# Last walk of a graph network kernel: a sixth of the one-hots is made one stage earlier, and the blocks' loads change engine

## The reference

```python
def gat_conv(x, W, att_src, att_dst, b, src, dst):
    n = x.shape[0]
    h = (x @ W).reshape(n, H, C)               # H = 2 heads, C = 64
    loops = jnp.arange(n, dtype=src.dtype)
    s = jnp.concatenate([src, loops])
    d = jnp.concatenate([dst, loops])
    a_s = jnp.einsum('nhc,hc->nh', h, att_src)
    a_d = jnp.einsum('nhc,hc->nh', h, att_dst)
    e = jax.nn.leaky_relu(a_s[s] + a_d[d], NEG_SLOPE)
    m = jax.ops.segment_max(e, d, num_segments=n)
    p = jnp.exp(e - m[d])
    denom = jax.ops.segment_sum(p, d, num_segments=n)
    alpha = p / (denom[d] + 1e-16)
    out = jax.ops.segment_sum(h[s] * alpha[:, :, None], d, num_segments=n)
    return out.reshape(n, H * C) + b
...
h = jax.nn.relu(gat_conv(x, W1, ...) + x @ Wsk1 + bsk1)
out = gat_conv(h, W2, att_src2, att_dst2, b2, src, dst) + h @ Wsk2 + bsk2
...
x = _layernorm(x + out)
```

## Time and profile before

| | us |
|---|---|
| median of 3 runs | 5302.19 |
| lowest and highest run | 5302.08, 5308.24 |
| span of the profiled execution | 5296.6 |
| busy: POOL, DVE, PE, ACT | 3515.2, 3404.7, 3373.0, 2334.8 |
| the last walk, from its first one-hot to the last instruction | some 393 |

### The profile page before, as it was taken

One profiled execution on the slowest core, in us unless ns is written; L12 is line 12 of the kernel. 1 busy time (PEld: TensorE's weight loads), 2 busy tenths in 40 slices (PEclk: granted clock), 3 DMA queues, 4 the chain that ended last, 5 costly groups with the idle time before them and its releaser, 6 DMA issues. The chain is left out here.

```text
span 5296.6 us, 96022 instructions
## 1 busy us (share of the span) xinstructions
PE 3373.0 (64%) x21145; PEld 2475.7 (47%) x21146; DVE 3404.7 (64%) x12799; ACT 2334.8 (44%) x6751; POOL 3515.2 (66%) x4335
## 2 busy tenths in 40 slices
PE   0027677677768869996959999962000899531566
PEld 0027666576756534441216666742000777420465
DVE  6984466554448857777848888863260888651777
ACT  0015466576657734442327888840000444200466
POOL 3870288676745567763748888867576555574999
PEclk9999899899989989997979999985555999855788
DMA  2123466598989862210113444435111999451576
GB/s 75 39 74 107 138 207 207 167 270 240 262 220 286 265 245 53 53 45 18 38 52 125 138 143 141 140 110 140 36 41 38 299 293 293 148 145 42 172 223 200
DMA packets 593103, 784.79 MB, mean 148 GB/s; under 512 B 138946, under 2 KB 362870, under 8 KB 592330
## 3 DMA queue, kind: packets, MB, share of 16 engines
q1 hardware_dynamic: 431734, 533.20, 32.7%
q0 software_dynamic: 62848, 112.43, 8.8%
q10 hardware_dynamic: 98328, 137.22, 7.1%
HBM read 470.23 MB, written 317.95 MB: 149 GB/s over the span
## 5 line engine op out<-in xcount | busy, mean ns | idle before, releaser
L2884 POOL TENSOR_SCALAR n_hot<-node_of,d_krel 128x256 f32<-128x256 f32 x396 | 381.1, 982 | 65.4 <-ACTq L2940 65.4
L1332 ACT ACTIVATE n_r<-n_r,n_shift,n_rstd 128x128 f32<-128x128 f32 x784 | 321.6, 480 | 79.0 <-POOL n_shift L1323 73.0
L1047 PE MATMUL e_bank<-x_rows,e_hot 128*128 x1584 | 197.6, 282 | 231.3 <-DVE e_hot L1020 184.1
L1003 POOL DMA_INDIRECT x_rows<-x,d_other_i x196 | 260.3, 1328 | 118.6 <-POOLq L102 59.2
L2912 PE MATMUL n_bank<-h_rows,n_hot 128*128 x1584 | 240.2, 320 | 146.1 <-POOL n_hot L2884 146.1
L684 POOL DMA_INDIRECT agg<-e_msg,e_put_i x196 | 194.2, 991 | 165.9 <-DVEq L713 114.6
L2912 PEld LDWEIGHTS n_bank<-h_rows,n_hot 128*128 128x128 f32 x1584 | 227.9, 231 | 159.1 <-issue 159.0
L1047 PEld LDWEIGHTS e_bank<-x_rows,e_hot 128*128 128x128 f32 x1584 | 185.4, 192 | 243.7 <-issue 243.7
L1332 ACT ACTIVATE n_o<-n_y_ps,n_shift,n_rstd 128x128 f32<-128x128 f32 x784 | 292.6, 453 | 13.0 <-POOL n_shift L1619 12.8
L615 POOL DMA_INDIRECT agg_dst<-e_rows,e_put_i x196 | 195.2, 996 | 101.9 <-issue 59.4
L2505 POOL TENSOR_TENSOR n_u<-n_u 128x512 f32<-128x512 f32 x98 | 124.5, 1271 | 205.7 <-DVE n_u L2452 205.7
(11 more groups left out here) (522 smaller groups left out, 11631.2 us busy)
## 6 DMA issues: line engine op xcount, KB each, us to landing
n_ag<-agg_dst SPq DMA_DIRECT2D x196, 264.0 KB, 2.9
n_hs<-h SPq DMA_DIRECT2D x196, 264.0 KB
n_xs<-x SPq DMA_DIRECT2D x196, 256.0 KB, 4.4
agg_dst<-e_ev SPq DMA_DIRECT2D x196, 132.0 KB
y<-n_o ACTq DMA_DIRECT2D x98, 264.0 KB, 2.7
e1a_fed<-y SPq DMA_DIRECT2D x196, 132.0 KB
m<-e1a_ev SPq DMA_DIRECT2D x196, 132.0 KB
e1b_fed<-m SPq DMA_DIRECT2D x196, 132.0 KB
```

The lines of the kernel that those rows point to most:

```text
L1003: pool.indirect_dma_start(out=rows[:, c, 0:fetched], out_offset=None, in_=table, in_offset=bass.IndirectOffsetOnAxis(ap=e.other_i[:, c:c + ...
L1047: ins = pe.matmul(bank[:, bass.ds(to + h * width, summed)], hot[:, s, k, h * P:(h + 1) * P], flat_rows[:, bass.ds(row, summed)], start=Fal ...
L1332: ins = act.activation(out[:, g, 0:D], r[:, g, :], ACT.Identity, bias=shift[:, g:g + 1], scale=rstd[:, g:g + 1])
L2884: ins = pool.tensor_scalar(hot[:, i // STEPB % HOTS, i % STEPB, :], keep.node_of[:, :], e.krel[:, i:i + 1], None, ALU.is_equal)
```

## The change

In the first part of `edge_shares` VectorE also makes, for each batch n, the one-hot of the batch's first step, in a ring of three buffers (`SPARES`). SyncE stores it to `spare_hots` in DRAM. In `walk_last` GpSimd skips the first step of each batch, SyncE fetches it into `hot[:, s, 0, :]` once `steps_done` frees the place, and TensorE also waits for `spare_in`. SyncE has no other work there: `load` and `close` are ScalarE's, whose lags are `close` 6, `begin` 2, `load` 0, `take_root` 7, `store` 9, `apply` 8.

```diff
 edge_shares, SyncE and VectorE:
+                    def store_spare(n):
+                        sp.wait_ge(spare_made, n + 1)
+                        sp.dma_start(spare_hots[n], spare[:, n % SPARES, :]).then_inc(spare_out[n % SPARES], 16)
...
+                        if n >= SLICES_IN:
+                            store_spare(n - SLICES_IN)
+                    for n in range(slices - SLICES_IN, slices):
+                        store_spare(n)
+                    for n in range(SPARES):
+                        sp.wait_ge(spare_out[n], 16 * (slices // SPARES))
...
+                        if n >= SPARES:
+                            dve.wait_ge(spare_out[n % SPARES], 16 * (n // SPARES))
+                        dve.tensor_scalar(spare[:, n % SPARES, :], keep.node_of[:, :], on_dst.krel[:, n * STEPB:n * STEPB + 1], None,
+                                          ALU.is_equal).then_inc(spare_made, 1)
 walk_last, GpSimd, TensorE, SyncE and ScalarE:
                     if i % STEPB == 0:
                         pool.wait_ge(steps_done, i + STEPB)
+                        continue
...
+                        pe.wait_ge(spare_in[s], turn * 16 + 16)
                         pe.wait_ge(hot_ready, turn * HOTS + s + 1)
...
-                run(sp, (0, load), (4, close))
+                with sp.Fori(0, BATCHES // HOTS) as turn:
+                    for s in range(HOTS):
+                        sp.wait_ge(steps_done, turn * (HOTS * STEPB) + (s + 1) * STEPB)
+                        sp.dma_start(hot[:, s, 0, :], spare_hots[bass.ds(turn * HOTS + s, 1)].squeeze(0)).then_inc(spare_in[s], 16)
...
+                def load(turn, s):
+                    upto(act, owned, turn, s, SLOT)
+                    act.dma_start(rows_of(hs, s), pair_rows(h4, turn, s)).then_inc(h_in[s % SLOT], 16)
+                    upto(act, begun, turn, s, SLOT, 2)
+                    act.dma_start(rows_of(ss, s), pair_rows(s4, turn, s)).then_inc(s_in[s % SLOT], 16)
...
+                    act.wait_ge(steps_done, ends[2 * (s % 2) + 1] & 511)
+                    act.sem_inc(closed, 1)
...
-                run(act, (0, begin), (PAST, begin_past), (5, take_root), (7, store), (6, apply))
+                run(act, (6, close), (2, begin), (0, load), (PAST + 2, begin_past), (7, take_root), (9, store), (8, apply))
```

More of the change, by code:

```diff
@@ L2602, with edge_shares @@
 SUMMED = D + GAT_HEADS
-def edge_shares(nc, keep, name, e, on_dst, krel_rows, h, a_nodes, values_edges, shares_edges, rows, share):
+SPARES = 3
+def edge_shares(nc, keep, name, e, on_dst, krel_rows, h, a_nodes, values_edges, shares_edges, rows, share, spare_hots):
     values = 2 * GAT_HEADS
@@ L2619, in edge_shares @@
             hot = ph.sb("hot", [P, 2, 2, SLICE * P], BF16)
+            spare = ph.sb("spare", [P, SPARES, TILE])
+            spare_made, spare_out = ph.sem("spare_made"), [ph.sem(f"spare_out{n}") for n in range(SPARES)]
             found, turned = ph.sb("found", [P, values, STEPS]), ph.sb("turned", [P, values, len(STEP_BLOCKS), P])
@@ L2850, in pair_rows, with walk_last @@
     return a.rearrange("(b t p h) d -> b p t h d", t=2, p=P, h=2)[bass.ds(turn * LAST_TURN + s, 1)].squeeze(0)
-def walk_last(nc, keep, e, rows, share, s4, h4, out):
+assert SLICE == STEPB and BATCHES % SPARES == 0
+def walk_last(nc, keep, e, rows, share, s4, h4, out, spare_hots):
     with Phase(nc, "n4") as ph:
@@ L2866, in walk_last @@
             ph.sem(n) for n in ("owned", "added", "taken", "together", "rooted", "scaled", "shifted", "normed", "go"))
+        spare_in = [ph.sem(f"spare_in{s}") for s in range(HOTS)]
         s_in, h_in, stored = ([ph.sem(f"{n}{s}") for s in range(SLOT)] for n in ("s_in", "h_in", "stored"))
@@ L2940, in _, with close @@
                 act.sem_inc(steps_done, HOTS * STEPB)
+                ends = []
+                def load(turn, s):
[3 more added lines that the diff above has]
+                    act.dma_start(rows_of(ss, s), pair_rows(s4, turn, s)).then_inc(s_in[s % SLOT], 16)
+                def close(turn, s):
+                    if s % 2 == 0:
+                        ends[:] = nc.values_load_multi_w_load_instructions(
+                            e.close[0:1, bass.ds(turn * (2 * LAST_TURN) + 2 * s, 4)], engines=[mybir.EngineType.Activation], min_val=0,
+                            max_val=(1 << 31) - 1, skip_runtime_bounds_check_because="walk_tables counts steps")[1]
+                    act.wait_ge(steps_done, ends[2 * (s % 2) + 1] & 511)
+                    act.sem_inc(closed, 1)
                 def begin(turn, s):
@@ L3086, in gnn @@
     s4 = dram("s4", (NPAD, ROW))
+    spare_hots = dram("spare_hots", (BATCHES, P, TILE))
     krel_rows = nc.dram_tensor("krel_rows", (STEPS, P), BF16, kind="Internal").ap()
@@ L3127, in gnn @@
         with nc.sbuf_tensor("h_rows", [P, J, ROW], F32) as rows, nc.sbuf_tensor("share", [P, GAT_HEADS, J], F32) as share:
-            edge_shares(nc, keep, "e4", to_dst, on_dst, krel_rows, h4, a4, values_edges, shares_edges, rows, share)
-            walk_last(nc, keep, on_dst, rows, share, s4, h4, out)
+            edge_shares(nc, keep, "e4", to_dst, on_dst, krel_rows, h4, a4, values_edges, shares_edges, rows, share, spare_hots)
+            walk_last(nc, keep, on_dst, rows, share, s4, h4, out, spare_hots)
 def kernel(**inputs):
```

## The result

The changed kernel takes 5357.21 us (median of 4 runs, 5352.31 to 5363.96) against 5303.3 for the kernel before on the same chip: a ratio of 1.0101, 95% interval 1.0087 to 1.0116. It is slower by 1%, where 5362 us and "slower" were forecast.

What follows compares the result with a forecast made beforehand. GpSimd was taken as the bound, a ScalarE-VectorE circle close behind; lengthened to 4.22 us a block, the walk gives +57.4, with +3 first stage and -0.9 first batch +59.5 us: 5362 us, range 5346 to 5392 (5297 to 5392 with rivals).

Steps and rivals of the forecast that it cites:

- The bound: Last walk: GpSimd sets the pace, 3.60 us a block; a circle of ScalarE and VectorE, 3.53, runs 0.07 inside it.
- The loads: ScalarE in the walk: two load issues between `begin` and the root lengthen the circle by 0.55 to 0.73 us; 0.73 taken.
- VectorE beside an idler GpSimd: Walk: VectorE's four-element shift runs faster when GpSimd is less busy, -0.04 us a block.
- `close`: ScalarE in the walk: passing on the count costs 0 to 0.2 us a block, taken as 0.
- The first stage: Value-spreading stage: VectorE's 66 new one-hots slow GpSimd's gathers, +3 us, about 20 us at the far end.
- First batch: Start of the walk: the first batch is ready one one-hot sooner, -0.9 us.
- The drain: End of the kernel after the last `begin`: stays as it is, 22.6 us, having no loads in it.
- The lower end of the range: Root at +1.10 and nothing in the first stage: 4.08 us a block, +44 us, 5346 us.
- the issues hide: Rival: the root does not feel the two load issues, the circle stays 3.53, 5298 us; chance 0.11.
- GpSimd's share is paid out: Rival: the circle follows GpSimd's pace, so 59 us come off, 5246 us; chance 0.07 together with a smaller form at 5283.
- The late count: Rival: `close` passes its count on only after the applies, 5.33 us a block, 5464 us; chance 0.04.

Runs made afterwards that it cites:

- x3: Kernel before with only one of six one-hots made in the earlier stage and fetched; loads and `close` stay on SyncE: 5286.8 us, ratio 0.9976.
- x7: Kernel before with `take_root` put ahead of `begin` in ScalarE's order, `begin_past` also waiting for TensorE's last batch but one: 5304.3 us, ratio 0.9985.
- x4: Kernel before with only `close` moved to ScalarE: 5302.0 us, ratio 1.0001.
- x5: Changed kernel with `take_root` put ahead of `begin` in ScalarE's order, `begin_past` also waiting for TensorE: 5320.5 us, ratio 1.0025.
- x9: Changed kernel with ScalarE's order made `close`, `load` (lag 1), `take_root`, `begin`, store, apply, and the added wait in `begin_past`: 5255.8 us, ratio 0.9906.
- x2: Kernel before with only the load issues moved to ScalarE, between `begin` and the root: 5352.1 us, ratio 1.0102.
- x8: Changed kernel with `load` (lag 1) moved between `close` and `begin` in ScalarE's order: 5290.6 us, ratio 0.9964.
- x6: x3 with `take_root` put ahead of `begin` in ScalarE's order, `begin_past` also waiting for TensorE: 5246.2 us, ratio 0.9872.
- x1: Changed kernel with the loads given back to SyncE, `close` staying on ScalarE: 5288.6 us, ratio 0.9977.

## Why the prediction was right

**The bound.** A circle of ScalarE and VectorE stood close behind GpSimd's pace: right, and shown from both sides by x3 and x7. Its links, in us, as forecast and as the mean of the 11th to the 90th block:

| link | forecast, before to after | before | after | x3 |
|---|---|---|---|---|
| `begin` to the root | 0.55 to 1.28 | 0.55 | 1.20 | 0.55 |
| root to the reciprocal | 0.31 to 0.31 | 0.31 | 0.33 | 0.31 |
| reciprocal to the addition | 1.94 to 1.90 | 1.98 | 1.89 | 1.84 |
| the addition | 0.65 to 0.65 | 0.65 | 0.65 | 0.65 |
| to the next `begin` | 0.08 to 0.08 | 0.10 | 0.11 | 0.10 |
| sum | 3.53 to 4.22 | 3.59 | 4.19 | 3.46 |

The 3.53 is that of one block. In the mean the circle of the kernel before takes as long as GpSimd's six one-hots, so there was no gap of 0.07 us between the two, and what x3 gains (3.59 to 3.46) is what VectorE's link gives back (1.98 to 1.84). Why the two ran in step is not shown.

**The loads.** +0.55 to +0.73 us a block, taken as 0.73: the root moved by 0.65 (single blocks lie near 1.15 and 1.22). The gap behind an issue was taken from an apply behind the store's issue, 0.18. But there the root's activation stood just ahead of the apply, from 5041.32 on the earlier trace rows. Behind the last load the root follows the issue's end by 0.05, and in the changed kernel the apply follows the store's issue by 0.05 as well (5104.09 to 5104.14).

**VectorE beside an idler GpSimd.** -0.04 was forecast, and its link is 0.08 shorter (1.98 to 1.89). The shift's median fell from 0.306 us to 0.146 (the profile after: 141/146/429 ns). GpSimd's idle time is only a part of the reason, since in x7 GpSimd never stops and the shift is as short:

```profile
L3019 DVE SCALAR_TENSOR_TENSOR n_shift<-n_mv,n_rstd x98: 143/145/561, 4952.9 to 5300.5; 128x4 f32<-128x4 f32 x98
```

What goes with it is where in a one-hot the shift starts. Take the 6th to the 93rd shift of each of the 13 profiles: the 326 that start 0.1 to 0.3 us after the start of a one-hot take 0.305 us in the mean, the 174 that start beside none 0.145, and the 156 that start 0.6 us or more into one 0.153 (the other 488 lie between or in the first 0.1 us, and are mixed). In the kernel before 68 of 88 started in the bad place, in the changed kernel 19, in x7 5.

The error of the root (-0.08) and that of VectorE's link (-0.04) have the same sign; the start at 3.53 in place of 3.59 and longer gaps (+0.03) have the other. So the sum is 4.19 and not 4.22. Over the whole walk, whose first and last blocks are shorter, it is 4.16, and the 93 intervals grew by 387.0 - 334.4 = 52.6 us where 57.4 was the sum.

**`close`.** Taken as free; 3.0 us of waits in the whole walk, and x4 gives 1.0001. In the changed kernel the count goes out 2.26 us behind `begin` in the mean, where near 2.3 was estimated, and so before the applies end: the four run from 1.83 to 3.48 us behind `begin` in the mean.

**The first stage.** +3 forecast, 0 found. The price of a one-hot on VectorE was bounded by 280 and 424 ns and is 353; the gathers' 260 us did not change.

**The rest.** First batch: -0.8 (from the last gather to the fifth `begin`, 102.6 to 101.8), near the forecast -0.9. That is partly luck: in x3, x5 and x9 the same stretch is 97.6 to 98.1 us, and why is not shown. The drain shrank by 1.4 us, forecast as unchanged. Sum of the change: 52.6 + 0 - 0.8 - 1.4 = +50.4 us. The span grew by 59.7, and the 9.3 between the two are the late start of the stage. The profiles as a whole show that the change need not be its cause: the first gather starts between 4575.8 and 4586.9 us in all of them, at 4586.1 in x7, whose code differs from the kernel before in ScalarE's program of the last stage alone. So the forecast of 5362 is as near as it is to 5357 with some luck: its own terms overshoot by 9 us, and the medians differ by 54. The lower end of the range has a slip: its 4.08 leaves out the -0.04 that the forecast and the upper end have. With it the bound is 4.04 us a block, 5342 us in place of 5346.

**The rivals.** That the issues hide is out (x2), though it holds one place further on (x8). With the same work and the same two issues a block the change is at 1.0101 and x8 at 0.9964: what tells the two apart is the instruction that stands behind the issues. That GpSimd's share is paid out is out for this order, and true once the root is moved (x6). The late count is out.

## What to carry to other kernels

When the chain that ended last names one full engine, look among the others for a wait that repeats every turn and add up the circle it belongs to, over many turns and not one; if the sum is within some per cent of the engine's pace, relieving the engine buys little: 0.14 of 0.60 us a block here. Before giving a transfer's issue to a computing engine, find the instruction that will stand behind it: beside the applies, where the engine would wait for the addition anyway, two issues left the root at 0.55 us here (x8, 3.51 us a block against 3.50 in x1), and ahead of a short instruction that another engine waits for they cost, in every turn, what the activation before them did not cover: the root came 0.10, 0.65 and 1.15 us later with one, two and three of them. Two bounds that lie close together have to be removed together to show the whole gain: 16 and 4 us alone, 62 together here.

## What was not expected of the hardware

- The part ahead of the last two stages, the same code in every kernel, ends with the first gather, between 4575.8 and 4586.9 us. That spread of 11 us is larger than several of the effects here, so the text compares stages, not spans.
- VectorE's shift, four elements in each partition, takes 143 ns at least in the kernel before and 306 in the median, beside a GpSimd that never stops. In x7 GpSimd never stops either and the median is 145. It is slow, 0.305 us in the mean, where it starts 0.1 to 0.3 us after a one-hot of GpSimd has started, and takes 0.145 us where it starts beside none.
- In x6 the DMA engines moved 296 GB/s at a share of 0.97, and TensorE's granted clock was 1.00 where it was 0.87 before and 0.78 in the changed kernel. TensorE is no bound in any of them: it is busy 170 of 260 us in x6, 228 of 340 before and 210 of 340 in the changed kernel.
